# Four gathers in flight instead of threes, and the steps of two chunks drawn forward by five tiles

## The reference

```python
xn = layernorm(x)                       # x: (2, 1024, 128)
x = x + attention0(xn) + experts0(xn)
xn = layernorm(x)
x = x + attention1(xn) + experts1(xn)

def attention0(x):                      # 16 heads of 8 features, full softmax
    q, k, v = split_heads(layernorm(x) * ln_w + ln_b @ qkv_w.T + qkv_b)
    q, k = q / norm(q), k / norm(k)
    return x + softmax(q @ k.T * sqrt(8)) @ v @ out_w.T + out_b

def experts0(x):                        # 64 experts, top 3, 64 slots each, hidden 512, exact gelu
    gates = softmax(top3(x @ gate_w + gate_b))
    buf[expert, position] = x[token]
    y = gelu(buf @ w1 + b1) @ w2 + b2
    return sum over the 3 experts of a token: gate * y[expert, position]

def attention1(x):                      # RWKV-v4: a recurrence over time, per feature
    r, v, k = split(x @ W_rvk.T)
    return (sigmoid(r) * wkv_scan(-exp(decay), first, k, v)) @ W_out.T

def experts1(x):                        # 8 experts, top 2, hidden 256, relu
    return sum over e of gate_e * (relu(x @ W1[e] + b1[e]) @ W2[e] + b2[e])
```

## Time and profile before

| | |
|---|---|
| runs, us | 526.62, 525.47, 521.34 |
| median, us | 525.47 |
| profiled execution, span, us | 525.06 |
| busy share PE, ACT, DVE, POOL | 94%, 71%, 58%, 27% |
| mean granted TensorE clock | 0.976 of full |

### The profile page before, as it was taken

One profiled execution on the slowest core, in us unless ns is written; L12 is line 12 of the kernel. 1 busy time (PEld: TensorE's weight loads), 2 busy tenths in 40 slices (PEclk: granted clock), 3 DMA queues, 4 the chain that ended last, 5 costly groups with the idle time before them and its releaser, 6 DMA issues.

```text
span 525.1 us, 11527 instructions
## 1 busy us (share of the span) xinstructions
PE 494.3 (94%) x4696; PEld 270.8 (52%) x4696; DVE 303.1 (58%) x790; ACT 375.1 (71%) x464; POOL 144.1 (27%) x133
## 2 busy tenths in 40 slices
PE   6977999999999999999998999999899999999996
PEld 5874223443455455445444232333467766767775
DVE  6799899434343343343330126367937983994895
ACT  3967988786978878978888989888535625553641
POOL 4078000303203203203000445425550755400120
PEclk8997999999999999999998999999899999999999
DMA  5200000565487877977362511100100110000000
GB/s 148 82 1 1 2 1 2 157 216 181 163 238 243 282 243 218 313 238 233 126 201 60 152 32 31 32 1 21 37 6 0 35 38 11 22 0 1 21 1 20
DMA packets 38542, 50.01 MB, mean 95 GB/s; under 512 B 3581, under 2 KB 20250, under 8 KB 38490
## 3 DMA queue, kind: packets, MB, share of 16 engines
q1 hardware_dynamic: 35524, 43.84, 25.4%
q0 software_dynamic: 2560, 5.25, 5.1%
q10 hardware_dynamic: 406, 0.20, 0.1%
HBM read 45.07 MB, written 4.19 MB: 94 GB/s over the span
## 4 chain that ended last, share of the span: by engine, by line
PE 50%; ACT 17%; DVE 6%; issue 5%; DVEq 0%
ACT region_b L564 11%; PE bank L1361 11%; PE scores L1609 9%; PE bank L1618 9%; PE scores L1347 5%; PE bank L1407 4%; PE bank L1395 3%; ACT xn L570 2%; PE bank L1417 2%; PE bank L1478 2%; DVE region_a L1067 2%; ACT L564 2%; ACT L570 2%; DVE base L1078 1%; PE bank L1372 1%
## 5 line engine op out<-in xcount | busy, mean ns | idle before, releaser
L564 ACT ACTIVATE region_b<-scores 128x1024 f32<-128x1024 f32 x256 | 242.4, 1045 | 51.8 <-PE scores L1347 51.6
L1361 PE MATMUL bank<-region_b 128*16 128x256 f32 x2048 | 149.0, 391 | 0.0
L1347 PE MATMUL scores<-region_b 32*128 32x512 f16 x512 | 83.0, 389 | 14.2 <-ACT region_b L564 14.0
L626 ACT ACTIVATE region_b<-scores,small_cols 128x512 f32<-128x512 f32 x64 | 43.6, 685 | 50.3 <-PE scores L1609 50.3
L388 POOL DMA_INDIRECT region_a<-xn_rows,slot_token x32 | 32.5, 1016 | 160.8 <-DVE h_rows L908 108.0
L1361 PEld LDWEIGHTS bank<-region_b 128*16 128x16 f32 x2048 | 42.0, 96 | 57.9 <-issue 42.6
L1618 PEld LDWEIGHTS bank<-region_a,region_b 128*128 128x128 f32 x512 | 62.2, 192 | 15.5 <-issue 15.3
L1347 PEld LDWEIGHTS scores<-region_b 32*128 32x128 f16 x512 | 20.8, 91 | 92.4 <-ACT region_b L564 68.9
L1618 PE MATMUL bank<-region_a,region_b 128*128 128x128 f32 x512 | 62.5, 275 | 0.0
L1609 PE MATMUL scores<-x_rows,region_a 128*128 128x512 f32 x128 | 62.3, 610 | 0.0
L1078 DVE SCALAR_TENSOR_TENSOR base<-bank,g,base 128x128 f32<-128x128 f32 x128 | 36.0, 344 | 28.0 <-PE bank L1618 27.6
(11 more groups left out here) (243 smaller groups left out, 590.6 us busy)
## 6 DMA issues: line engine op xcount, KB each, us to landing
region_a<-in_L_ffn_w SPq DMA_DIRECT2D x64, 512.0 KB, 5.3
region_a<-in_L_ffn_b SPq DMA_DIRECT2D x17, 128.0 KB, 7.2
slot_out<-slots_io SPq DMA_DIRECT2D x8, 256.0 KB, 7.7
region_a<-in_L_attn_x SPq DMA_DIRECT2D x4, 256.0 KB, 4.5
xn_rows<-xn SPq DMA_DIRECT2D x1, 1024.0 KB, 5.1
region_a<-in_L_ffn_W SPq DMA_DIRECT2D x1, 1024.0 KB, 5.9
out<-base SPq DMA_DIRECT2D x4, 256.0 KB, 2.3
region_a<-xn_rows,slot_token POOLq DMA_INDIRECT x32, 3.7
```

The costliest lines, as they stand in the source:

```text
L564: a.activation(PR[:, n % PBUF, 2 * h:2 * h + 2, :], S[:, 2 * h:2 * h + 2, :], ACT.Exp, scale=SCALE).then_inc(s["exp_done"], 1)
L626: a.activation(HS[:, e % 2, k], ps[2 * (e % 2) + k][:], ACT.Relu, bias=COL[:, HC1 * e + k:HC1 * e + k + 1]).then_inc(s["relu_done"], 1)
L1347: last = mm(S[:, j], KT[head, hg, keys], QT[head, hg, BLK * c:BLK * c + BLK], start=True, stop=True)
L1361: last = mm(AV[32 * j:32 * j + VW, cols], VA[:, tile, HG * (g % NHG) + j, :], PR[:, st % PBUF, j, cols], start=(st == 0 and half == 0), st ...
```

## The change

Three things are changed.

1. The gathers use four semaphores in turn ("lanes") instead of one for each chunk. Gather n waits until gather n - 4 has landed, through all chunks; the wait for a row tile's three, and the one between chunks 0 and 1, are gone. DVE and POOL now wait for all four lanes before they combine a chunk.
2. Every step of chunk 0, and the steps of chunk 1 that stood in the loop, stand five tiles earlier on PE, DVE and ACT (so does `MIXED`). `mixed(0)` goes from tile 127 to 122.
3. `normed(1)` and `normed_cols(1)` go from the first step of the tail into tiles 124 and 125.

```diff
+    LANES = 4
-    MIXED = (94, 109, 111, 112, 120, 125)
+    MIXED = (89, 104, 106, 107, 115, 120)
-        gathered = [sem(f"gathered{c}") for c in range(NC)]
+        gathered = [sem(f"gathered{i}") for i in range(LANES)]
             def gather(c):
                 for t in range(CH * c, CH * c + CH):
-                    if t > CH * c:
-                        pool.wait_ge(gathered[c], 16 * TOPK * (t - CH * c))
                     for k in range(TOPK):
+                        n = TOPK * t + k
+                        if n >= LANES:
+                            pool.wait_ge(gathered[n % LANES], 16 * (n // LANES))
                         g.indirect_dma_start(YGS[c % 2][:, t - CH * c, k, :], None, slot_out, ...
-                                             bounds_check=SLOTS - 1, oob_is_err=True).then_inc(gathered[c], 16)
+                                             bounds_check=SLOTS - 1, oob_is_err=True).then_inc(gathered[n % LANES], 16)
             def combine(c):        # on POOL; on DVE alike
-                pool.wait_ge(gathered[c], 16 * TOPK * CH)
+                for i in range(LANES):
+                    pool.wait_ge(gathered[i], 16 * TOPK * CH // LANES * (c + 1))
             gather(0)
-            pool.wait_ge(gathered[0], 16 * TOPK * CH)
             gather(1)
...
-                if n == 98:
+                if n == 93:
                     combine(0)
-                if n == 100:
+                if n == 95:
                     x1_norm(0)
...
-                if n == 121:
+                if n == 116:
                     combine(1)
-                if n == 122:
+                if n == 117:
                     time_mix_end(0)
...
-                if n == 125:
+                if n == 120:
                     finish(0)
+                if n == 124:
+                    normed(1)
```

More of the change, by code:

```diff
@@ L633, in _ @@
                     a.activation(GE[:], GE[:], ACT.Exp).then_inc(s["gexp_ready"], 1)
-                if n == 113:
[L635 to L640, removed]
+                if n == 108:
+                    gate_exps(0)
+                if n == 109:
+                    receptance(0)
+                if n == 110:
+                    state_exps(0)
+                if n == 113:
                     output_exps(0)
@@ L926, in combine @@
             def combine(c):
-                dve.wait_ge(gathered[c], 16 * TOPK * CH)
+                for i in range(LANES):
+                    dve.wait_ge(gathered[i], 16 * TOPK * CH // LANES * (c + 1))
                 if c:
@@ L1139, in _ @@
                         moe_in(G + 1)
+                if n == 88:
+                    attention_rows(0)
                 if n == 93:
-                    attention_rows(0)
-                if n == 98:
                     combine(0)
-                if n == 100:
+                if n == 95:
                     x1_norm(0)
+                if n == 97:
+                    x1_scale(0)
                 if n == 102:
-                    x1_scale(0)
-                if n == 107:
                     normed_cols(0)
-                if n == 110:
+                if n == 105:
                     gates_in(0)
@@ L1153, in _ @@
                     time_mix(0)
-                if n == 112:
+                if n == 107:
                     values_in(0)
-                if n == 113:
+                if n == 108:
                     gates(0)
-                if n == 114:
+                if n == 109:
                     time_mix_first(0)
-                if n == 116:
+                if n == 111:
                     gates_cols(0)
                     time_mix_states(0)
-                if n == 117:
-                    attention_rows(1)
-                if n == 118:
-                    time_mix_out(0)
-                if n == 121:
-                    combine(1)
+                if n == 112:
+                    attention_rows(1)
+                if n == 113:
+                    time_mix_out(0)
+                if n == 116:
+                    combine(1)
+                if n == 117:
+                    time_mix_end(0)
+                if n == 119:
+                    x1_norm(1)
+                if n == 120:
+                    x1_scale(1)
                 if n == 122:
-                    time_mix_end(0)
-                if n == 124:
-                    x1_norm(1)
+                    mixed(0)
                 if n == 125:
-                    x1_scale(1)
-                if n == 127:
-                    mixed(0)
+                    normed_cols(1)
             evacuate(NG - 1)
@@ L1180, in _ @@
                 accumulate(e // E1, e % E1)
-                if e == 0:
-                    normed_cols(1)
                 for y in range(1, NC):
@@ L1580, in _ @@
                     slots_in(0)
-                if n == 92:
+                if n == 87:
                     attention_cols(0)
-                if n == 94:
+                if n == 89:
                     attention_out(0)
+                if n == 101:
+                    normed(0)
+                if n == 104:
+                    keys_logits(0)
                 if n == 106:
-                    normed(0)
-                if n == 109:
-                    keys_logits(0)
+                    values_in(0)
+                if n == 107:
+                    receptance(0)
+                if n == 110:
+                    gates_out(0)
                 if n == 111:
-                    values_in(0)
-                if n == 112:
-                    receptance(0)
+                    attention_cols(1)
                 if n == 115:
-                    gates_out(0)
-                if n == 116:
-                    attention_cols(1)
+                    attention_out(1)
                 if n == 120:
-                    attention_out(1)
-                if n == 125:
                     finish(0)
+                if n == 124:
+                    normed(1)
             for half in range(2):
@@ L1630, in _ @@
                 down2(e // E1, e % E1)
-                if e == 0:
-                    normed(1)
                 for y in range(1, NC):
```

## The result

The changed kernel takes 532.12 us (median of 4 runs, 531.34 to 534.0) where the kernel before takes 523.40 us (4 runs, 521.09 to 526.62): a ratio on record of 1.0144, 95% interval 1.0083 to 1.0205 (the two medians alone give 1.0167). It is slower. Runs of one kernel differ by several us, as falls of the clock come and go, a trace is of one run, and the ratios leave out runs more than 1.5% above the fastest of their kernel (two of four in e5, two of ten in e7). Slower is the side which the forecast held for the likelier of the two, but the time lies 0.9 us above the top of its range, so one of its steps has to be found wrong.

What follows compares the result with a forecast made beforehand. PE, busy 94%, and ACT were taken to bound the loop together, with time changing only where an engine waits. From 525.06 us, minus 1.8 gains, plus 2.8 PE wait, plus 1.4 clock fall: 527.5 us, range 522.0 to 531.2.

Steps and rivals of the forecast that it cites:

- The gathers and the late copy: Chunk 0: gathers 1.31 us apart, combining at 307.8 us, tile 96's copy late, PE waiting 2.8 us.
- Their shorter time I cost at nothing: Later gathers, chunks 1 to 3: they lie beside other work, so their shorter time was counted as zero.
- The base, 525.06 us: Starting time of the sum: the profiled span of the kernel before, 0.41 us under the median.
- The fall of the clock: After PE's wait before tile 96's values: clock likely falls to the 1.2 GHz level, costing 1.4 us (bounds 0 and 1.4).
- The gains: Loop end and tail: 1.3 us net in the loop plus some 0.5 us in the tail, 1.8 us together.
- the 0.98 us wait before `finish(0)`: End of the old loop: PE waits for DVE's last multiplication of `time_mix_end(0)`, then the clock falls.
- The 48 passes: Passes over the values at the loop's end: 4.47 us before, about 3.1 us expected at the full clock.
- DVE in time at `finish(0)`: Late loop: DVE between 2.9 us early and 0.9 us late, taken as 1 us early with no wait.
- The tail: Start of the tail: it loses the transposes of `normed(1)`, gaining some 0.5 us.
- the rival of unseen falls: Tail: clock falls of 1.4 us each that come or go with the phase, among things unseen; chance 0.03.
- DVE holding up the gathers: Chunk 0's gathers: busy DVE slows three issues, combining 2.3 us later, time 529.8 us; chance 0.05.

Runs made afterwards that it cites:

- e5: The changed kernel with its steps moved but the gathers in threes as before (lanes undone): 537.04 us, ratio 1.0144 to the kernel before.
- e7: The changed kernel with the second mixture's weights loaded only after `combine(0)`: 526.04 us, ratio 1.0005 to the kernel before.
- e4: The kernel before with the four gather lanes and no step moved: 532.14 us, ratio 1.0134 to the kernel before.
- e2: The changed kernel with POOL's combining of chunk 2 held until DVE has done `mixed(0)`: 527.51 us, ratio 1.0054 to the kernel before.
- e1: The changed kernel with DVE copying n = 96 first and combining chunk 0 behind it: 524.99 us, ratio 1.0017 to the kernel before.
- e3: The changed kernel with chunk 0 combined behind tile 96's copy and POOL's combining of chunk 2 held until `mixed(0)`: 523.44 us, ratio 0.9936 to before.
- e8: The kernel before with four lanes, old steps, and POOL's combining of chunk 2 held until `mixed(0)`: 522.56 us, ratio 0.9957 to before.
- e6: The changed kernel with 20 useless PE matmuls ahead of tile 96's values: 527.39 us, ratio 1.0048 to the kernel before.
- e9: The changed kernel with chunk 0 combined behind tile 96's copy, POOL's chunk 2 combining held until `mixed(0)`, later second-mixture weights: 521.89 us, ratio 0.9942 to before.

## Why the prediction missed

- **The gathers and the late copy: right.** Pace 1.31 us, only the fifth waits, combining at 19.25 us (19.5), PE's wait 3.25 us (2.8). From the issue of the twelfth to the combining are 2.86 us; the estimate of 2.15 us from the Trainium skill's page DMA: Bandwidth & Descriptors, section Anatomy of one DMA, is too low here too.
- **"Their shorter time I cost at nothing": wrong, and the step that failed.** I asked who would wait for the later gathers, and not whom POOL's work behind them would meet. The rows could have told: before, `x1_scale(1)` ran from 376.29 to 379.86 us, and POOL multiplied at 382.14, 23.6 us after the first gather of chunk 2 (358.51). Six us off that stretch put it at 376 us, on top of `x1_scale(1)`, as e4 shows; and where the steps are drawn forward, `mix(0)`, which POOL does ahead of those gathers, comes forward with them, so that the two still meet. Price: 4.6 us between the medians of the changed kernel and e2, 0.9% by the ratios; in the traces 3.5 us of the loop (after against e2) or 2.5 (e1 against e3). That is the whole of what lies between the forecast's 527.5 us and the measured 532.12.
- **The base, 525.06 us: right by luck.** It is a span that I let stand as a time. In every run of the experiments the time is 1.7 to 1.8 us more than the span, so as a time the sum would be some 529.2 us. But the profiled execution was also long for its kernel: a run of the median time, 525.14 us, has a span of 523.4. The two errors cancel.
- **The fall of the clock: right in kind; its size is not settled.** I took one fall at 1.4 us. The trace has three, one of them behind the collision, and the first held until about 320.4 us. In the traces the loop grows by 3.67 us from before to e2, which has everything but the collision, and shrinks by 3.14 in e3, where PE waits for DVE at neither place: 6.8 us for wait and falls, where I had 4.2. But e2's trace is of its longest run. The medians of e2 and e3 differ by 4.1 us, the ratios by 1.2%, about 6 us.
- **The gains: not settled either.** By the medians e3 is 1.7 us under the kernel before, as the forecast's 1.8. By the traces it is 3.1 us in the loop instead of 1.3. Of them 1.9 came as the fall at 376 us went (e8 against before, 90.70 to 92.63; e8 still has the 0.98 us wait before `finish(0)`, so that wait does not always bring a fall), and 1.2 are the steps' own. The 48 passes take 2.78 us at the full clock, not 3.1, and `normed(1)` left ACT idle for 0.24 us, not 0.40: 0.5 us of the 1.8 that the forecast lacks here; the rest is not worked out. So e2's 527.5 us agrees with the forecast either with its terms near their sizes, as the medians have it, or with two that are off by some 2 us each and cancel, as the traces have it.
- **DVE in time at `finish(0)`: right**, no wait there or before tile 120's values.
- **The tail: -0.5 us right**, and a fall of the clock less (430 us) that I had left to the rival of unseen falls: -2.07 together. e2, with the same steps, has a tail of 143.72 us; this one comes and goes.

What stays open: why the clock fell near 349 us after, and not in e1. Both have the same work there, with a wait of 1.00 us of PE for ACT ahead of it, 8.5 us earlier in e1. In e2 the clock falls there too; before and in e3, e6, e7 and e9 it does not, with the same wait (0.99 to 1.00 us). No run tells it apart.

## What to carry to other kernels

When transfers get faster, follow the engine that issued them to its next piece of work, and look which operations of other engines will now run beside it: a margin of 2.3 us, that nobody had written down, decided here. Before drawing a step forward on an in-order engine, find the small copy behind it that a busier engine waits for, and let that copy go first. Two costs that each look like 1% are told apart by taking away one at a time, and then both, to see whether they add.

## What the runs showed of the hardware

In these traces a GpSimd `tensor_tensor` on SBUF holds up VectorE's operations on SBUF until it ends, however small they are: 0.16 us became 2.64 beside a multiplication of 2.75, and 1.13 beside additions of some 1.3 us. VectorE's operations on a PSUM bank beside the same GpSimd work took their usual 0.48 and 1.13 us. The Trainium skill's page SBUF — State Buffer, section SBUF: two separate sides, calls the shared pair of ports an exclusive lock for a whole instruction, taken by a GpSimd operation as well as by a VectorE operation that has two SBUF inputs or runs in a two-port mode. For two SBUF inputs (line 966) this trace agrees. Line 962 of e4 has one such tensor and was held up too (2.68 us instead of 0.17); no run shows in which mode it ran. I had cited that section for the opposite direction only, DVE holding up the gathers, which did not happen to chunk 0: its twelve took 1.00 or 1.01 us each.

With 2 MB of weights on the DMA engines, the first gathers landed late enough to hold up the fifth for 2.24 us; without them it waited for nothing (0.30 us, the usual gap).
